# A fused two-layer attention and mixture-of-experts kernel: eleven tiles of the second expert layer get a table of their own and start before the last router groups are finished

## The chip, the cores and the metric

One core of a Trainium2 chip runs the whole kernel. The metric is the device time of one execution in microseconds (us). Three executions of the kernel before took 702.17, 703.75 and 704.6 us, a median of 703.75 us.

## The reference

32 sequences of 128 tokens with 128 features go through two layers. Each layer is a gated cross-attention (16 heads) and a gated mixture of 8 experts, both on a layer-normed copy of the running sum `x`:

```python
x = x + tanh(g_xattn[0]) * L0_xattn(layernorm(x), ctx, ...)
x = x + tanh(g_ffn[0])   * L0_ffn(layernorm(x), ...)         # one expert per token
x = x + tanh(g_xattn[1]) * L1_xattn(layernorm(x), ctx, ...)
x = x + tanh(g_ffn[1])   * L1_ffn(layernorm(x), ...)         # two experts per token

# L1_ffn
probs = softmax(xt @ gate_w.T); top_w, top_i = top_k(probs, 2)
top_w = top_w / (top_w.sum(-1) + 1e-9)
h = gelu(xt @ w1[e] + b1[e]); out_e = h @ w2[e] + b2[e]      # 128 -> 512 -> 128
out = sum over the two chosen experts of top_w * out_e
```

The change is about the last two lines of `x`: the end of the second attention and the second expert layer. A token's two experts are known only when its attention is done, and rows of one expert are computed together.

## The kernel before

The kernel is written by hand for the five engines; every engine has its own program, in order, and semaphores join them. Nothing is scheduled by a planner.

**Attention slots.** The batch is cut into 16 pairs of sequences. `pair_slots` runs slots p = -4, -3, ... and in slot p each engine does one step of several pairs: maxima of the scores of pair p+1 (TensorE, VectorE), scores and exponentials of pair p, values of pair p-1, the division, the new `x` and its statistics for pair p-2 (VectorE; the reciprocal root of the variance on GpSimd, L599 to L602), and for pair p-3 the normalised copy N (ScalarE, L717), its transpose (L824) and the router's logits (L954, L765). The second layer's slots run to p = 20, so slots 17 to 20 only bring the last pairs home.

**Router groups.** `GROUPS` cuts the pairs into six groups. A group's routing (`choose`, steps 0 to 19 on VectorE, `rank_group` on TensorE, one exponential on ScalarE) gives every token the two rows (SLOT) at which it stands among its experts' rows. GpSimd then writes the rows there with one indirect DMA for each 128 tokens and choice, `dispatch` (L628), 64 in all, to the tensor `dispatched`.

**The table.** After the last group `tables_by_first_row` (VectorE, L1389 to L1426, with three steps on TensorE) makes the list of 39 tiles of 256 rows: first row (TBL 0), expert (TBL 1) and the number of groups that must have been stored (TBL 2). The tiles are ordered by the group that fills their first row.

**Expert slots.** `tile_slots` runs slots i = -2 to 39. In slot i TensorE transposes the rows of tile i+1 (L824), does the hidden layer of tile i (L1057) and the output layer of tile i-1 (L1074). SyncE loads a tile's rows (L503) when its groups are stored. ScalarE copies the transposed rows (L791) and does gelu (L802). VectorE copies the weights (L1573), makes the rows' addresses and weights (L1580 to L1588), and for the output y adds the bias (L1598) and scales by the router's weight (L1601, twice). GpSimd sends y back by two indirect DMAs (L663). Transposed rows and y alternate between two PSUM banks each. At the end the rows are fetched back for chunks of tokens, summed (L1622) and added to x (L1625).

## Time and profile before

| | us |
|---|---|
| median of three executions | 703.75 |
| the profiled execution | 701.35 |
| its span in the profile | 699.5 |
| TensorE busy | 554.2 (79%) |
| VectorE busy | 507.9 (73%) |
| ScalarE busy | 359.4 (51%) |
| GpSimd busy | 308.2 (44%) |

A row of busy times gives the stretch, its length, then busy us (and instructions) of PE, PEld, DVE, ACT and POOL, the granted clock, the DMA share and GB/s. A row of the timeline gives start, duration, engine, source line, operation, output and inputs, and in brackets the idle time before it with what ended it. PEld is TensorE's weight load, SPq the DMA queue of SyncE. PEclk is the granted clock of TensorE as a share of 2.4 GHz. The execution lies 1.85 us above its own span and 2.4 us below the median.

### The profile page before, as it was taken

How to read it: one execution, taken by the hardware profiler on the slowest of the kernel's cores; microseconds unless marked ns; L12 is line 12 of the kernel's file. 1: busy time of each engine (PE TensorE's matmuls, PEld its weight loads, DVE VectorE, ACT ScalarE, POOL GpSimd, SP SyncE). 2: the span in 40 equal slices, each digit the busy share in tenths (PEclk: the TensorE clock that was granted, in tenths of full speed). 3: DMA queues.
4: the chain of work that ended last, by engine and by line, in shares of the span. 5: the costliest groups of instructions: out<-in, count | busy, mean ns of one | idle time of the engine just before them, and what ended most of it. 6: DMA issues, size and time to landing. Idle time of an engine off the chain costs nothing.

```text
span 699.5 us, 17510 instructions
## 1 busy us (share of the span) xinstructions
PE 554.2 (79%) x5770; PEld 452.3 (65%) x5770; DVE 507.9 (73%) x1617; ACT 359.4 (51%) x860; POOL 308.2 (44%) x431
## 2 busy tenths in 40 slices
PE   6789999998840118997779989898843999999991
PEld 4667777776630007886656767676532999999991
DVE  5998889888348884553789999999755555666662
ACT  2177777776723104551256767677721555555550
POOL 5512233221110017755664225575777445555553
PEclk9899999999975557999989999999975999999996
DMA  5354434433010002342546545442113222344333
GB/s 179 89 142 132 138 108 140 148 110 85 19 56 22 0 4 75 107 97 80 147 144 182 164 147 169 140 119 85 42 43 93 66 77 68 119 145 126 109 126 105
DMA packets 99864, 72.59 MB, mean 104 GB/s; under 512 B 13272, under 2 KB 93272, under 8 KB 99752
## 3 DMA queue, kind: packets, MB, share of 16 engines
q1 hardware_dynamic: 88496, 53.64, 26.3%
q0 software_dynamic: 6816, 14.10, 6.7%
q10 hardware_dynamic: 4464, 3.73, 1.8%
q8 instruction: 48, 0.79, 0.5%
q14 instruction: 40, 0.33, 0.2%
HBM read 42.14 MB, written 29.85 MB: 103 GB/s over the span
## 4 chain that ended last, share of the span: by engine, by line
PE 54%; DVE 22%; issue 9%; ACT 5%; DMA 4%; POOL 3%; SPq 1%; POOLq 0%; DVEq 0%; ACTq 0%
PE bank L1057 14%; PE bank L1074 10%; PE bank L824 7%; DVE MX L1247 5%; PE bank L861 5%; PE bank L992 5%; PE bank L845 4%; PE bank L1067 3%; DVE PT L1478 2%; ACT OT L760 2%; PE bank L941 2%; ACT XT_HL_WR L736 2%; DVE XN L1290 1%; PE bank L908 1%; PE bank L897 1%
## 5 line engine op out<-in xcount | busy, mean ns | idle before, releaser
L703 ACT ACTIVATE PT<-bank 128x512 f32<-128x512 f32 x256 | 151.9, 597 | 92.2 <-PE bank L845 91.7
L1247 DVE TENSOR_REDUCE MX<-bank 128x4 f32<-128x512 f32 x256 | 172.5, 680 | 20.1 <-PE bank L861 18.0
L861 PE MATMUL bank<-KS,QS_N 96*128 96x128 f16 x1024 | 102.9, 224 | 12.5 <-DVE MX L1247 7.2
L663 POOL DMA_INDIRECT returned<-PT,META_ROW x78 | 79.4, 1018 | 66.4 <-DVE PT L1601 54.2
L1057 PE MATMUL bank<-XGT,XT_HL_WR 128*128 128x256 f32 (+1 forms) x468 | 103.5, 359 | 1.6 <-issue 1.0
L861 PEld LDWEIGHTS bank<-KS,QS_N 96*128 96x128 f16 x1024 | 76.0, 102 | 35.7 <-DVE MX L1247 14.5
L845 PE MATMUL bank<-QS_N,KS 98*128 98x512 f16 x256 | 97.5, 386 | 0.7 <-ACT PT L703 0.3
L1057 PEld LDWEIGHTS bank<-XGT,XT_HL_WR 128*128 128x128 f32 x468 | 79.5, 198 | 14.1 <-issue 7.2
L1074 PEld LDWEIGHTS bank<-WALL,HT 128*128 128x128 f32 x624 | 75.6, 192 | 2.6 <-issue 0.6
L628 POOL DMA_INDIRECT dispatched<-N,SLOT x64 | 63.3, 989 | 31.2 <-issue 15.1
L1074 PE MATMUL bank<-WALL,HT 128*128 x624 | 76.1, 275 | 0.2 <-issue 0.2
L802 ACT ACTIVATE HT<-bank,XT_HL_WR 128x256 f32<-128x256 f32 x156 | 63.9, 471 | 21.4 <-PE bank L1057 21.4
L791 ACT ACTIVATE XGT<-bank 128x128 f32<-128x128 f32 (+1 forms) x78 | 25.8, 330 | 94.6 <-PE bank L824 90.8
L992 PE MATMUL bank<-PT,VA 128*32 128x128 f32 x2048 | 70.2, 278 | 0.1
L650 POOL DMA_INDIRECT PT<-normed,LIST x39 | 37.8, 969 | 71.3 <-DVE LIST L1546 59.8
L1573 DVE COPY XT_HL_WR<-WALL 128x512 f32 (+1 forms) x78 | 35.3, 453 | 42.2 <-issue 27.5
L992 PEld LDWEIGHTS bank<-PT,VA 128*32 128x32 f32 x2048 | 52.7, 111 | 18.0 <-issue 11.5
L599 POOL TENSOR_SCALAR MINUS<-MV_N 128x2 f32<-128x2 f32 x32 | 7.6, 237 | 120.9 <-DVE MV_N L1130 120.6
L1598 DVE TENSOR_TENSOR PT<-bank,WALL 128x256 f32<-128x256 f32 x39 | 16.6, 425 | 42.6 <-PE bank L1074 42.6
L615 POOL DMA_INDIRECT HT<-returned,SLOT x32 | 31.6, 989 | 18.4 <-DMA returned<-PT 9.8
L824 PE MATMUL bank<-CONST,PT 128*128 128x128 f32 x117 | 27.2, 288 | 11.1 <-issue 5.1
L717 ACT ACTIVATE N<-X,OFFSET_N,RSTD_N 128x128 f32<-128x128 f32 x64 | 27.8, 483 | 7.9 <-POOL OFFSET_N L602 7.8
(240 smaller groups left out, 994.1 us busy)
## 6 DMA issues: line engine op xcount, KB each, us to landing
spread<-XT_HL_WR SPq DMA_DIRECT2D x96, 128.0 KB
QS_N<-spread SPq DMA_DIRECT2D x128, 48.0 KB
KS<-spread SPq DMA_DIRECT2D x32, 192.0 KB
PT<-dispatched SPq DMA_DIRECT2D x39, 132.0 KB, 2.1
WALL<-in_w SPq DMA_DIRECT2D x8, 578.0 KB
CT<-in_ctx SPq DMA_DIRECT2D x32, 128.0 KB, 2.6
returned<-PT SPq DMA_DIRECT2D x39, 64.0 KB
WALL<-in_w ACTq DMA_DIRECT2D x8, 256.0 KB, 2.8
```

What stands on the lines that cost most here:

```text
L628: pool.indirect_dma_start(xs[:, :], bass.IndirectOffsetOnAxis(ap=SLOT[:, k, b:b + 1], axis=0), N[:, b, :], None).then_inc(SCAT[d.s], 16)
L650: pool.indirect_dma_start(XG6[:, i % 6, 0:D], None, normed[:, :], bass.IndirectOffsetOnAxis(ap=LIST[:, i:i + 1], axis=0)).then_inc(XA[i % ...
L663: pool.indirect_dma_start(ys[1][:, :], bass.IndirectOffsetOnAxis(ap=META_ROW[:, a.f, c:c + 1], axis=0), YS[:, a.f, c, :], None).then_inc(S ...
L703: nc.scalar.activation(PT[:, c, 4 * g:4 * g + 4, :].rearrange("p j q -> p (j q)"), ST[i % 2][:, :], ACT.Exp, scale=SCALE[layer]).then_inc( ...
L802: last = nc.scalar.activation(HT[:, a.u, m, :], bank[2 * a.u + m // 2][:, TILE * (m % 2):TILE * (m % 2) + TILE], ACT.Gelu, bias=WR[:, a.t, ...
L824: return nc.tensor.transpose(to, of, ident[0:n, 0:n])
L845: nc.tensor.matmul(ST[i % 2][:, :].rearrange("p (j q) -> p j q", j=J), KS[0:98, x.r, g, c * P:(c + 1) * P], QS[0:98, x.r, J * g:J * g + J, ...
L861: last = nc.tensor.matmul(MB[i % 2][:, j * P:(j + 1) * P], QS[0:96, m.r, J * g + j, c * P:(c + 1) * P], KS[0:96, m.r, g, c * P:(c + 1) * P ...
L992: last = nc.tensor.matmul(PA[32 * g:32 * g + 32, 256 * c + P * (j // 2):256 * c + P * (j // 2) + P], VA[:, b.r, c, head(g, j), :], PT[:, c ...
L1057: last = nc.tensor.matmul(bank[2 * a.u + m // 2][:, n * (m % 2):n * (m % 2) + n], WR[:, a.t, m * P:(m + 1) * P], XGT[:, a.u, 0:n], start=T ...
L1074: last = nc.tensor.matmul(bank[6 + a.u][:, c * D:(c + 1) * D], HT[:, a.u, m, c * P:(c + 1) * P], WALL[:, bass.ds(r + (W1COLS[1] + m * D), ...
L1247: V.tensor_reduce(out=MX[:, m.u, 2 * J * g + c:2 * J * (g + 1):2], in_=MB[i % 2][:, :].rearrange("p (j k) -> p j k", j=J), op=ALU.max, axi ...
```

## The change

1. The second layer's attention slots end at p = 16. What stood in slots 17 to 20 (normalised copy, transpose and logits of the last two pairs, the last pair's division, routing of groups 4 and 5) is run by a function `drain(i)` of each engine ahead of expert slots -2 to 9.
2. The groups are (0,3), (3,3), (6,3), (9,2), (11,3), (14,2). The first three groups fill at least 11 whole tiles (`EARLY`). These have their own table, made in attention slots 15 and 16 from the counts of three groups. The other 28 tiles' table is made in `drain(7)` to `drain(9)`. SyncE waits for groups 0 to 2 before tile 0 and for all before tile 11.
3. GpSimd writes the 12 blocks of group 4 before the first y and the 8 blocks of group 5 behind the y of tile 1.
4. In slots 15 and 16 the statistics of pair p-2 move ahead on VectorE, and ScalarE normalises a pair at the end of the slot in which its statistics are made.
5. ScalarE scales y in place of VectorE, one slot later; y has one PSUM bank (PA) and the transposed rows have one (PG), where there were two each.
6. TensorE and VectorE load the table's register ahead of the slot's waits.

```diff
-GROUPS = ((0, 3), (3, 3), (6, 3), (9, 3), (12, 2), (14, 2))
+GROUPS = ((0, 3), (3, 3), (6, 3), (9, 2), (11, 3), (14, 2))
+EARLY_GROUP = 2
+IN_SLOTS = 4
+EARLY = -(-(sum(GROUPS[EARLY_GROUP]) * 4 * P - E * (TILE - 1)) // TILE)
-            for p in range(-4, PAIRS + (3, 5)[layer]):
+            for p in range(-4, PAIRS + (3, 1)[layer]):
 # SyncE, second_experts
+                sp.wait_ge(av_done, 4 * PAIRS - 1)
                 sp.wait_ge(tables_ready, 2)
+                stored_groups(0, EARLY_GROUP + 1)
                 for i in range(TILES[1]):
+                    if i == EARLY:
+                        sp.wait_ge(tables_ready, 3)
+                        stored_groups(EARLY_GROUP + 1, len(GROUPS))
-                    sp.wait_ge(groups_done, need)
 # GpSimd, second_experts
-                confirm(Group(len(GROUPS) - 1))
+                deviations(LAST)
+                rest_of_stores(4, 0, 12)
                 for i in range(TILES[1]):
-                    pool.wait_ge(y_kept, a.g + 1)
+                    if i == 2:
+                        rest_of_stores(5, 0, 8)
+                    pool.wait_ge(y_scaled, i + 1)
 # ScalarE
+            def drain(i):
+                if i == -2:
+                    keep_transposed(BEFORE_LAST)
+                if i == 0:
+                    shares(Group(4))
+                    keep_logits(BEFORE_LAST)
+                if i == 1:
+                    normalise(LAST)
+                if i == 2:
+                    keep_transposed(LAST)
+                if i == 3:
+                    keep_logits(LAST)
+                if i == 5:
+                    shares(Group(5))
+            def scaled(a):
+                act.wait_ge(y_kept, a.g + 1)
+                for c in range(2):
+                    last = nc.scalar.activation(YS[:, a.f, c, :], YS[:, a.f, c, :], ACT.Copy, scale=META_W[:, a.f, c:c + 1])
+                last.then_inc(y_scaled, 1)
 # TensorE
+                    if layer == 1 and p == PAIRS - 1:
+                        table_order(0)
                     scores_for_maxima(7)
                     scores(a, 3)
...
+            def drain(i):
+                if i == -2:
+                    transposed(BEFORE_LAST)
+                if i == 0:
+                    logits(1, BEFORE_LAST)
+                if i == 1:
+                    rank_group(Group(4))
+                if i == 2:
+                    transposed(LAST)
+                if i == 3:
+                    logits(1, LAST)
+                if i == 6:
+                    rank_group(Group(5))
+                    table_counts(1)
+                if i == 8:
+                    table_order(1)
+                if i == 9:
+                    table_rows(1)
-                        pe.wait_ge(y_kept, before(a.g - 1))
+                        pe.wait_ge(y_kept, before(a.g - 1 + layer))
-                                    last = nc.tensor.matmul(bank[6 + a.u][:, c * D:(c + 1) * D], HT[:, a.u, m, c * P:(c + 1) * P],
+                                    last = nc.tensor.matmul(PA[:, c * D:(c + 1) * D], HT[:, a.u, m, c * P:(c + 1) * P],
 # VectorE
+            def drain(i):
+                if i == -1:
+                    steps(4, range(7))
+                if i == 0:
+                    divide(1, LAST)
+                    add_attention(LAST)
+                    second_stats(LAST)
+                    steps(4, range(7, 11))
+                if i == 1:
+                    steps(4, (11, 13, 14, *WEIGHTS))
+                if i == 4:
+                    steps(5, range(7))
+                if i == 5:
+                    steps(5, range(7, 12))
+                if i == 6:
+                    steps(5, (13, 14, *WEIGHTS))
+                if i == 7:
+                    table_keys(1)
+                if i == 8:
+                    table_values(1)
+                    table_places(1)
+                if i == 9:
+                    table_columns(1)
-                        for c in range(2):
-                            last = V.tensor_scalar(out=YS[:, a.f, c, :], in0=YS[:, a.f, c, :], scalar1=META_W[:, a.f, c:c + 1],
-                                                   scalar2=None, op0=ALU.mult)
```

Where the instructions stand, in three places. First TensorE between the attention and the first expert tiles. `PLACE,VALUES` is the table, `N` the normalised copy, `WG,NT` the logits, `MASKG` and `SHARE` the ranks of a group, `CONST,PT` the transposes of a tile's rows, `XGT` a hidden layer. Before:

```order
L954 MATMUL bank<-WG,NT 128x8 x2
L978 MATMUL bank<-MASKG,BEFORE 128x32
L979 MATMUL bank<-SHARE,ONES 128x32
L981 MATMUL bank<-MASKG,ONES 128x32
L981 MATMUL bank<-MASKG,ONES 128x24
L981 MATMUL bank<-MASKG,ONES 128x16
L981 MATMUL bank<-MASKG,ONES 128x8
L1031 MATMUL bank<-MASKG,ONES 128x56
L824 MATMUL bank<-CONST,ONE 128x128
L1037 MATMUL bank<-PLACE,VALUES 128x39 x4
L824 MATMUL bank<-CONST,PT 128x128 x4
L1057 MATMUL bank<-XGT,XT_HL_WR 128x256 x4
```

Now, from the last values of the attention on:

```order
L1058 MATMUL bank<-PT,VA 32x128 x16
L901 MATMUL bank<-CONST 128x128 x3
L896 MATMUL bank<-CONST,OT 128x128 x4
L896 MATMUL bank<-CONST,N 128x128 x2
L896 MATMUL bank<-CONST,PT 128x128 x2
L1075 MATMUL bank<-WG,NT 128x8 x2
L896 MATMUL bank<-CONST,PT 128x128 x2
L1190 MATMUL bank<-XGT,XT_HL_WR 128x256 x4
L1083 MATMUL bank<-MASKG,BEFORE 128x48
```

The first hidden layer has moved ahead of the ranks of groups 4 and 5 and of the whole table; the transpose of pair 14's copy N stands directly before the first tile's rows.

Second, GpSimd at the same place (`MINUS` to `OFFSET_N` are the four small steps of one pair's normalisation). Before, all of it from the last two normalisations:

```order
L602 TENSOR_TENSOR OFFSET_N<-MINUS,RSTD_N 128x2
L628 DMA dispatched<-N,SLOT 34816x132 x6
L599 TENSOR_SCALAR MINUS<-MV_N 128x2
L600 TENSOR_SCALAR VE_N<-MV_N 128x2
L601 TENSOR_TENSOR RSTD_N<-VE_N,EXPO 128x2
L602 TENSOR_TENSOR OFFSET_N<-MINUS,RSTD_N 128x2
L628 DMA dispatched<-N,SLOT 34816x132 x22
L663 DMA returned<-PT,META_ROW 18176x128 x78
```

Now, from pair 14's normalisation on:

```order
L590 TENSOR_TENSOR OFFSET_N<-MINUS,RSTD_N 128x2
L644 DMA dispatched<-N,SLOT 34816x132 x2
L587 TENSOR_SCALAR MINUS<-MV_N 128x2
L588 TENSOR_SCALAR VE_N<-MV_N 128x2
L589 TENSOR_TENSOR RSTD_N<-VE_N,EXPO 128x2
L590 TENSOR_TENSOR OFFSET_N<-MINUS,RSTD_N 128x2
L644 DMA dispatched<-N,SLOT 34816x132 x12
L688 DMA returned<-PT,META_ROW 18176x128 x4
L644 DMA dispatched<-N,SLOT 34816x132 x8
L688 DMA returned<-PT,META_ROW 18176x128 x74
```

The last 20 blocks now stand around the y of tiles 0 and 1; group 3's are all ahead of the last normalisation.

Third, ScalarE in expert slots 4 to 6 (`HT` gelu, `PT<-PT,META_W` the scaling, `EXG` the exponential of group 5), where there were only copies and gelu:

```order
L853 ACTIVATE XGT<-bank 128x256
L877 ACTIVATE PT<-PT,META_W 128x128 x2
L866 ACTIVATE HT<-bank,XT_HL_WR 128x256 x4
L809 ACT_TABLE_LOAD
L809 ACTIVATE EXG<-SHX 128x36
L853 ACTIVATE XGT<-bank 128x256
L877 ACTIVATE PT<-PT,META_W 128x128 x2
L866 ACT_TABLE_LOAD
L866 ACTIVATE HT<-bank,XT_HL_WR 128x256 x4
```

Two loads of ScalarE's tables and the scalings have come in between the gelus.

## Rows read from the trace of the kernel before

**Rows 1.** Page, part 2: 40 slices of the span, tenths

```profile
PE   6789999998840118997779989898843999999991
PEclk9899999999975557999989999999975999999996
```

**Rows 2.** Busy time by engine in slot 14, the hand-over and the expert loop

```profile
486.00:494.30 8.30, 7.32 (x112) 5.06 (x111) 7.11 (x17) 6.01 (x13) 6.08 (x9) 1.00 0.14 45
...
506.80:537.70 30.90, 9.28 (x70) 7.48 (x67) 18.38 (x96) 4.29 (x13) 23.38 (x27) 0.62 0.18 58
543.60:685.50 141.90, 141.90 (x992) 133.94 (x992) 85.93 (x343) 75.24 (x186) 76.44 (x76) 1.00 0.35 106
```

**Rows 3.** Chain of waits in order of time, 506 to 534 us

```profile
506.94 1.07 POOL dispatched L628
...
533.21 2.14 DMA PT<-dispatched
```

**Rows 4.** Timeline of PE: attention slots 14 to 16, first tiles, steady state

```profile
486.06 0.27 PE L824 MATMUL bank<-CONST,MX 128*32 128x128 f32 x1
...
494.33 0.27 PE L824 MATMUL bank<-CONST,MX 128*32 128x128 f32 x1
...
500.31 0.38 PE L845 MATMUL bank<-QS_N,KS 98*128 98x512 f16 x1
...
508.26 0.60 PE L824 MATMUL bank<-CONST,OT 128*128 128x128 f32 x4
...
537.72 3.62 PE L1057 MATMUL bank<-XGT,XT_HL_WR 128*128 128x256 f32 x8
...
541.54 1.89 PE L1057 MATMUL bank<-XGT,XT_HL_WR 128*128 128x256 f32 x8
543.60 2.05 PE L1074 MATMUL bank<-WALL,HT 128*128 x16 [0.17 <-issue]
...
566.09 1.95 PE L1074 MATMUL bank<-WALL,HT 128*128 x16
567.88 0.38 PE L824 MATMUL bank<-CONST,PT 128*128 128x128 f32 x2
```

**Rows 5.** Timeline of POOL from slot 14 on

```profile
488.37 1.09 POOL L628 DMA_INDIRECT dispatched<-N,SLOT  x1 [0.56 <-issue]
489.76 0.96 POOL L628 DMA_INDIRECT dispatched<-N,SLOT  x1 [0.30 <-issue]
...
494.71 0.24 POOL L599 TENSOR_SCALAR MINUS<-MV_N 128x2 f32<-128x2 f32 x1 [0.20 <-DVE MV_N L1130]
...
496.11 0.19 POOL L602 TENSOR_TENSOR OFFSET_N<-MINUS,RSTD_N 128x2 f32<-128x2 f32 x1
```

**Rows 6.** Timeline of DVE: table, then one expert slot

```profile
524.57 0.21 DVE L1389 COPY BASE<-bank 128x56 f32<-128x56 f32 x1
...
528.02 0.16 DVE L1402 SCALAR_TENSOR_TENSOR ONE<-ONE 128x1 f32<-128x1 f32 x1
...
529.76 0.25 DVE L1415 TENSOR_SCALAR PLACE<-CONST,ONE 128x39 bf16<-128x39 f32 x1
...
531.33 0.20 DVE L1422 TENSOR_SCALAR TBL<-bank 128x39 int32<-128x39 f32 x1
...
564.46 0.42 DVE L1598 TENSOR_TENSOR PT<-bank,WALL 128x256 f32<-128x256 f32 x1 [1.06 <-PE bank L1074]
```

**Rows 7.** Granted clock, 1 us windows: fall and rise

```profile
514.00:515.00 1.00, 0.00 (x0) 0.00 (x0) 0.83 (x4) 0.00 (x0) 0.78 (x4) 0.60 0.16 55
...
541.00:542.00 1.00, 1.00 (x6) 0.81 (x5) 0.00 (x0) 0.99 (x4) 0.80 (x1) 0.74 0.70 189
```

**Rows 8.** Timeline of ACT: a normalised copy, and the load of gelu's table

```profile
516.02 0.88 ACT L717 ACTIVATE N<-X,OFFSET_N,RSTD_N 128x128 f32<-128x128 f32 x2 [3.21 <-POOL OFFSET_N L602]
...
539.72 1.28 ACT L802 ACT_TABLE_LOAD   x1 [1.37 <-PE bank L1057]
541.01 1.57 ACT L802 ACTIVATE HT<-bank,XT_HL_WR 128x256 f32<-128x256 f32 x4
```

More of the change, by code:

```diff
@@ L997, in attention_slot, with transposed, logits @@
                 return slot
+            def transposed(y):
+                pe.wait_ge(n_copied, y.g + 1)
+                pe.wait_ge(lg_kept, y.g)
+                for c in range(2):
+                    last = transpose(PF[:, 256 + c * P:256 + (c + 1) * P], N[:, y.b + c, 0:D])
+                last.then_inc(n_t, 1)
+            def logits(layer, y):
+                pe.wait_ge(n_kept, y.g + 1)
+                for c in range(2):
+                    last = nc.tensor.matmul(PF[:, 256 + E * c:256 + E * c + E], NT[:, c * P:(c + 1) * P],
+                                            WG[:, layer, :], start=True, stop=True)
+                last.then_inc(lg_done, 1)
@@ L1078, in expert_layer @@
                 pe.wait_ge(tables_ready, layer + 1)
-                tile_slots(layer, slot)
+                tile_slots(layer, slot, None, drain if layer else None)
             for layer in range(2):
@@ L1228, in slot @@
                     m, a, b, z, f, n = pair(1), pair(0), pair(-1), pair(-2), pair(3), pair(4)
+                    late = layer == 1 and p >= PAIRS - 1
                     def low_halves():
@@ new lines, in table_columns @@
+            def table_columns(part):
+                first, n = PARTS_OF_TILES[part]
+                these = slice(first, first + n)
+                chain.sync()
+                dve.wait_ge(ordered, part + 1)
+                read = (PG, PF)[part]
+                start, expert, filled = (read[:, 2 * P + k * n:2 * P + (k + 1) * n] for k in range(3))
+                link(V.tensor_copy(FILLED[:, 0, these], filled))
+                link(V.scalar_tensor_tensor(out=STARTF[:, these], in0=start, scalar=float(TILE), in1=FILLED[:, 0, these], op0=ALU.mult, op1=ALU.add))
+                link(V.tensor_copy(TBL[:, 0, these], STARTF[:, these]))
+                if part == 0:
+                    link(V.tensor_copy(TAKEN[:, :], read[:, 3 * P:3 * P + E]))
+                V.tensor_scalar(out=TBL[:, 1, these], in0=expert, scalar1=float(WCOLS[1]), scalar2=None,
```

395 lines of the change are left out of this document (238 added, 157 removed).

## The prediction

> **What bounds the kernel now.** I read the page first, then busy times by stretch, then the chain of waits, then each engine's timeline around the place that the change touches. The page's slices show TensorE nearly full in both attention layers and in the last quarter, with a hole between the second attention and the second expert layer, in which its clock also falls [rows 1]. The stretches put numbers on it: between the last values of the attention (506.8) and the first hidden layer (537.7) TensorE is busy 9.28 of 30.9 us at a granted clock of 0.62; from the first output layer (543.60) to the last (685.5) it is busy 141.90 of 141.90 us at 1.00 [rows 2]. So the expert loop is TensorE's: each of the 39 tiles is an output layer of 1.78 us (566.09 to the transposes at 567.88 [rows 4]), two transposes and a hidden layer, 3.73 us in all (141.9 us for 38 rounds), and nothing taken from another engine there shortens it. The hole belongs to a chain: in it GpSimd's dispatches and normalisations, then routing and table on VectorE, then SyncE's load of the first rows, which lands at 535.35 [rows 3]. What the change can win is the hole, some 31 us plus the slow start behind it.
>
> **When the first tiles can start.** I follow the new order engine by engine, with durations of before.
>
> Slot 14 gets group 3's routing, 14 small VectorE steps. VectorE is busy 7.11 of 8.3 us there [rows 2]; at some 0.2 us a step 2.0 of the 3 us fill idle time or overlap, and I take 0.8 us more for the slot. Bounds: 0 and 3.
>
> Slot 15 gets the early table. `table_keys` took 3.6 us (524.57 to 528.18) and `table_values` and `table_places` 1.8 (to 530.01) [rows 6]. VectorE's other work ahead of it in that slot (the split of the maxima, division, new x, statistics, weights of group 3: 15 instructions of 0.15 to 0.5 us) is some 4 us by my estimate, so the keys end 7.6 us after the slot's start at 494.33 [rows 4], at about 502 on the old clock. TensorE has `table_order(0)` in front of the last pair's scores 3, which ran at 500.31 [rows 4]: a new wait of about 2 us, behind which stand ScalarE's exponentials.
>
> The later wait is GpSimd's. Counting from its first dispatch of slot 14 at 488.37, 16 dispatches and the normalisations of pairs 12, 13 and 14 now stand in front of pair 14's OFFSET_N: 6 + 8 + 2 dispatches of 1.26 us (0.96 and 0.30 of issue) are 20.2 us, three normalisations of 1.7 us (494.71 to 496.30 and a start) are 5.1 [rows 5]. That is 513.7, where before the same step was done just ahead of the dispatch at 506.94 [rows 3]: group 3's eight dispatches were moved ahead of it. TensorE needs this copy before the first tile's rows, as the new order shows. The rows themselves are there: the early table's places are made in slot 15 and its columns, 1.3 us, behind two steps of TensorE in slot 16, by my estimate at about 508.7; from a finished table (531.53 [rows 6]) it was 1.7 us to SyncE's issue at 533.21 and 2.14 more to the landing [rows 3]: 512.5.
>
> From 513.7: ScalarE's copy 0.9 [rows 8], two transposes of N 0.45, two of the rows 0.4, ScalarE's copy of both 0.8, the logits 0.5, the next transposes 0.4; hidden layer 0 starts at about 516.9. Then 1.73, the ranks of group 4 0.5, transposes 0.4, hidden layer 1 1.73: the first output layer would start at 521.2 at full clock. But TensorE is idle for over 3 us before it and thin before that. In the run of before the transposes of 508.26 [rows 4] were the last work but for short bursts, and the clock went to 1.2 GHz inside 514 to 515; it came back inside 541 to 542, 4 us into steady work [rows 7], and hidden layer 0 took 3.62 us there where the next took 1.89 [rows 4]. I take half of some 4 us for it, 2.0 (bounds 0 and 4): 523.2. Against 543.60 the start is **20.4 us earlier**.
>
> **What the loop gets in return.** TensorE is full there, so everything it is given counts: one pair's transposes 0.45, its logits 0.5, ranks and counts 0.8, the table's two steps 0.6: **2.3 us**.
>
> VectorE waits 1.06 us for TensorE in a tile of before [rows 6] and is rid of the scaling, 0.5 us: about 1.5 us to spare. The drains of slots 4 and 5 fit (7 and 5 steps, 1.6 and 1.2 us); that of slot 6 (8 steps behind the ranks) leaves it 0.8 late. Slot 7 gives it 17 steps, 3.9 us, and slot 8 another 2.0. An output layer may be late only by what lies between the add that frees the y bank (564.46 + 0.42) and the next output layer (566.09), 1.2 us [rows 4, 6]. What is over is a stall of TensorE in slots 8 and 9: 3.9 + 0.8 - 1.5 - 1.2 is 2.0, less the 0.4 that TensorE itself loses there: **1.6 us** (bounds 0 and 4).
>
> Tile 11 is the seam. Its load waits for the late table and for group 5. The table is ready one us into `drain(9)`; SyncE's 1.5 and the transfer's 2.2 follow, and against TensorE's own need in slot 10 this is **2.9 us** late. GpSimd runs beside it to nearly the same end: group 4 may start at 521.3, 12 dispatches are 15.1, y of tiles 0 and 1 5.0, group 5 10.1: 551.5 and a landing of 1.5 at the most beyond the instruction (a load takes 2.14 from its issue), where the table is ready at about 555. Then y of tile 2 goes, and tile 10's addresses wait for it (eight buffers): 555.6, just in time.
>
> Costs taken at nothing: ScalarE's scaling (0.7 us a tile in an engine busy 75.24 of 141.90 us [rows 2]; if that cover went, gelu would be late and the price be per tile); register loads ahead of waits (TensorE has no gap to give back); one bank for the transposed rows (ScalarE's copy is done 1.5 us before the next transposes); the two loads of ScalarE's tables around group 5's exponential. For these the row shows 1.28 us, gelu right behind it at 541.01 [rows 8]: slot 5 then takes ScalarE 1.28 + 0.23 + 0.38 + 0.7 + 1.28 + 1.64 = 5.5 us, and it has 6.1 to 6.7 before TensorE wants the gelu. The Trainium skill, page "ScalarE: Activation LUTs", section "What ACT_TABLE_LOAD costs", speaks against this: every switch costs 2.66 us, for about 1.38 us of draining goes with the load. By that page slot 5 would take ScalarE some 8.3 us and TensorE would lose about 2 more. Before the one load in this trace no such drain shows.
>
> At the end ScalarE's scaling stands where two VectorE steps stood: 0.2 us.
>
> **Sum.** 20.4 - 2.3 - 1.6 - 2.9 - 0.2 = 13.4 us. The profiled execution was 701.35, so its like would be 688.0; the median of the runs shown stands 2.4 above it, and from 703.75 the forecast is **690.3 us**.
>
> **The rivals.**
>
> *Less is lost at the seam* (0.18). If the clock does not fall and VectorE's steps overlap as they do between the maxima, 2.0 and some 3 of the 4.5 us of stalls stay: 18.4 us, 685.3. For it: short steps cost little behind long ones. Against it: all steps in the drains depend on each other.
>
> *GpSimd's queue takes the seam* (0.23). Twenty dispatches and four y are 30 us in front of tile 2's y. Anything that makes them 0.2 us longer each, or starts group 4 later, comes out at tile 10's addresses and again in slots 11 and 12, while VectorE is held in order; ScalarE's dearer table switches belong here too. At 5 us: 695.3.
>
> *One bank for y* (0.05, the slower side). VectorE's add stands behind weights and addresses (1.85 us) in its slot. If gelu, behind ScalarE's new scaling, releases the weights so late that the add always comes those 1.85 us later, the next output layer waits 0.65 us in every tile: 39 tiles are 25 us, 715. It turns the sign from an add that comes 1.55 us late (1.2 of cover and 13.4 / 39). Against it: ScalarE is idle for half of each tile.
>
> *The early tiles do not start early* (0.04). If a wait in the new order ties tile 0 to something late, the last pair's work for instance, the hole stays and only its filling moves: 703, no change.
>
> **How the numbers follow.** 0.50 for the forecast, within about 687 to 694 by the bounds of the slot, the clock and the stalls. The range runs from the mean of the better case less a us to the seam case plus 2: 684 to 697.5; it leaves out the last two cases and the tails. A difference within 0.3% (2.1 us) cannot be told from none. Faster 0.91, same 0.04, slower 0.05.
>
> **What would show it.** Right: the first output layer at 520 to 525 of the span; N's copy of pair 14 released by GpSimd at about 514, with dispatches in a row before it; TensorE without a gap in the loop except 1 to 2 us around slots 8 and 9 (released by VectorE's add) and some 3 us before tile 11's transposes (released by the load of its rows); 3.73 us a tile from tile 12 on. Wrong: gaps in every tile; a first tile after 530; a stall of over 5 us at tile 10 or 11; or no stall there at all.

## The result, and the profile after

The changed kernel took 686.48, 689.23, 692.8 and 693.06 us, a median of **691.01 us**; four runs of the kernel before, 701.12 to 704.6, have a median of 702.96. The ratio is 0.9829 with a 95% interval of 0.9802 to 0.9857: faster by 12 us, where 690.3 was forecast. The profiled execution is the one of 692.8 us, 1.8 above the median. The page of the changed kernel, lines that answer to [rows 1] and the two groups of the expert loop:

```profile
span 691.1 us, 17399 instructions
...
PE   6789999999861106987769998899879989999991
...
PEclk8789999999995555999889999999968999999996
...
PE 49%; DVE 19%; issue 10%; ACT 7%; POOL 7%; DMA 7%; SPq 1%; POOLq 0%; ACTq 0%; DVEq 0%
...
L1190 PE MATMUL bank<-XGT,XT_HL_WR 128*128 128x256 f32 (+1 forms) x468 | 102.1, 356 | 0.2 <-issue 0.2
...
L1212 PE MATMUL bank<-WALL,HT 128*128 x624 | 76.7, 276 | 1.0 <-DVE PT L1826 1.0
```

The hole in TensorE's row has shrunk to a dent (8, 7), and a thin place of the loop has come in its stead. Busy times of slot 14, slot 16 and the loop from the first output layer to the last (they answer to [rows 2]):

```profile
489.10:498.10 9.00, 7.66 (x118) 5.19 (x117) 8.72 (x30) 6.24 (x14) 6.90 (x10) 1.00 0.15 49
507.50:518.50 11.00, 9.69 (x89) 6.51 (x87) 5.88 (x27) 5.11 (x12) 7.81 (x12) 0.50 0.27 75
526.30:676.50 150.20, 145.23 (x1010) 136.12 (x1008) 72.24 (x327) 100.35 (x271) 93.29 (x96) 0.99 0.36 108
```

Slot 14 opens with the transposes of the maxima at 489.12; before, it opened at 486.06. The three us are lost near the kernel's start, which the change does not touch: the third pair of the first attention layer has its maxima transposed at 49.69 us, before at 46.38, and the granted clock of 34 to 52 us is 0.86, before 1.00. This part differs from one execution to the next: in the profiles of the first four variants below slot 14 opens between 482.7 and 491.3. So I compare **from slot 14's start**:

| us | before | after | difference |
|---|---|---|---|
| slot 14's start to the first output layer (543.60; 526.28) | 57.54 | 37.16 | -20.38 |
| first output layer to the end of the last (685.51; 676.52) | 141.91 | 150.24 | +8.33 |
| from there to the end | 14.0 | 14.6 | +0.6 |
| slot 14's start to the end | 213.4 | 202.0 | -11.4 |

The hand-over in the timelines of PE, ACT, DVE and POOL (start, duration, engine, line, operation, in brackets the idle time ahead of it and what ended it):

```profile
506.25 0.32 PE L896 MATMUL bank<-CONST,ONE 128*128 128x128 f32 x1 [1.89 <-DVE ONE L1605]
...
514.12 1.93 PE L1058 MATMUL bank<-PT,VA 128*32 128x128 f32 x32 [0.69 <-ACT PT L728]
...
517.43 1.06 PE L896 MATMUL bank<-CONST,OT 128*128 128x128 f32 x4
518.58 0.66 PE L896 MATMUL bank<-CONST,N 128*128 128x128 f32 x2
...
521.05 3.20 PE L1190 MATMUL bank<-XGT,XT_HL_WR 128*128 128x256 f32 x8
...
517.61 0.88 ACT L793 ACTIVATE N<-X,OFFSET_N,RSTD_N 128x128 f32<-128x128 f32 x2 [0.89 <-POOL OFFSET_N L590]
...
512.01 0.17 DVE L1647 COPY FILLED<-bank 128x11 f32<-128x11 f32 x1 [3.73 <-PE bank L1111]
...
515.87 0.24 POOL L587 TENSOR_SCALAR MINUS<-MV_N 128x2 f32<-128x2 f32 x1 [0.54 <-DVE MV_N L1268]
...
517.38 0.20 POOL L590 TENSOR_TENSOR OFFSET_N<-MINUS,RSTD_N 128x2 f32<-128x2 f32 x1
...
527.23 1.09 POOL L644 DMA_INDIRECT dispatched<-N,SLOT  x1 [3.38 <-DVE N L1336]
```

ScalarE's copy of pair 14 waits for GpSimd, as forecast, and ends at 518.49. But TensorE, which is to transpose that copy, has only just finished its own work: its transposes at 518.58 stand behind others that also ended at 518.49. The clock had gone to 1.2 GHz behind the wait for the table's order at 506.25, and slot 16 took 11.0 us where it took 7.2 before. Two paths end together here. They are not quite apart either: GpSimd's dispatches were done at 515.34, and it then waited 0.54 us for pair 14's statistics, which VectorE could make only after its own wait of 3.73 us for TensorE's slow slot (512.01).

The seam, first in PE's timeline, then in the chain of waits, then in the view of the dispatching line:

```profile
552.44 0.32 PE L896 MATMUL bank<-CONST,ONE 128*128 128x128 f32 x1 [0.99 <-DVE ONE L1605]
...
554.89 2.05 PE L1212 MATMUL bank<-WALL,HT 128*128 x16 [0.18 <-DVE PT L1826]
...
558.83 1.95 PE L1212 MATMUL bank<-WALL,HT 128*128 x16
563.76 0.44 PE L896 MATMUL bank<-CONST,PT 128*128 128x128 f32 x2 [2.98 <-DMA PT<-dispatched]
564.04 3.01 PE L1190 MATMUL bank<-XGT,XT_HL_WR 128*128 128x256 f32 x8
566.84 2.54 PE L1212 MATMUL bank<-WALL,HT 128*128 x16
```

```profile
556.58 4.08 DMA dispatched<-N,SLOT
...
561.59 2.13 DMA PT<-dispatched
```

```profile
DMA to landing us min/median/max: 2.3/2.3/4.1
```

Group 5's last dispatch was issued at 556.58 and landed 4.08 us later, where the median from issue to landing is 2.3: SyncE could load tile 11 only then. TensorE waited 2.98 us and then ran its next hidden layer at half clock for part of the way (3.01 instead of 1.89, the output layer 2.54 instead of 1.95).

### The profile page after: what moved, and what is told of

It reads as the page before. It is cut to its first block, busy times and chain, and to the rows that moved or that the text cites. A ratio compares the mean times of both kernels' runs of the same rounds, so it can differ in the third digit from the quotient of the medians.

```text
span 691.1 us, 17399 instructions
## 1 busy us (share of the span) xinstructions
PE 554.3 (80%) x5751; PEld 453.2 (66%) x5751; DVE 487.8 (71%) x1575; ACT 383.4 (55%) x940; POOL 307.9 (45%) x431
## 3 DMA queue, kind: packets, MB, share of 16 engines
q10 hardware_dynamic: 4464, 3.73, 1.9%
## 4 chain that ended last, share of the span: by engine, by line
PE 49%; DVE 19%; issue 10%; ACT 7%; POOL 7%; DMA 7%; SPq 1%; POOLq 0%; ACTq 0%; DVEq 0%
PE bank L1190 9%; PE bank L1212 8%; PE bank L896 7%; PE bank L1058 6%; PE bank L934 5%; DVE MX L1396 5%; PE bank L917 5%; POOL dispatched L644 3%; DMA PT<-normed,LIST 2%; DVE PT L1708 2%; POOL PT L672 2%; ACT OT L781 2%; PE bank L1020 2%; ACT XT_HL_WR L761 2%; ACT PT L728 1%
## 5 line engine op out<-in xcount | busy, mean ns | idle before, releaser
L934 PE MATMUL bank<-KS,QS_N 96*128 96x128 f16 x1024 | 103.3, 225 | 14.6 <-DVE MX L1396 8.5
L1190 PE MATMUL bank<-XGT,XT_HL_WR 128*128 128x256 f32 (+1 forms) x468 | 102.1, 356 | 0.2 <-issue 0.2
L688 POOL DMA_INDIRECT returned<-PT,META_ROW x78 | 77.6, 994 | 51.5 <-ACT PT L877 36.3
L917 PE MATMUL bank<-QS_N,KS 98*128 98x512 f16 x256 | 99.2, 392 | 0.5 <-ACT PT L728 0.5
L1212 PEld LDWEIGHTS bank<-WALL,HT 128*128 128x128 f32 x624 | 76.3, 193 | 3.6 <-issue 1.6
L1212 PE MATMUL bank<-WALL,HT 128*128 x624 | 76.7, 276 | 1.0 <-DVE PT L1826 1.0
L1058 PE MATMUL bank<-PT,VA 128*32 128x128 f32 x2048 | 72.4, 284 | 0.7 <-ACT PT L728 0.7
L1058 PEld LDWEIGHTS bank<-PT,VA 128*32 128x32 f32 x2048 | 54.2, 113 | 19.8 <-issue 11.5
L738 ACT ACTIVATE XT_HL_WR<-bank 128x256 f32<-128x256 f32 x32 | 12.1, 379 | 35.7 <-PE bank L896 35.7
```

The costliest lines, as they stand in the source:

```text
L688: pool.indirect_dma_start(ys[1][:, :], bass.IndirectOffsetOnAxis(ap=META_ROW[:, a.f, c:c + 1], axis=0), YS[:, a.f, c, :], None).then_inc(S ...
L917: nc.tensor.matmul(ST[i % 2][:, :].rearrange("p (j q) -> p j q", j=J), KS[0:98, x.r, g, c * P:(c + 1) * P], QS[0:98, x.r, J * g:J * g + J, ...
L934: last = nc.tensor.matmul(MB[i % 2][:, j * P:(j + 1) * P], QS[0:96, m.r, J * g + j, c * P:(c + 1) * P], KS[0:96, m.r, g, c * P:(c + 1) * P ...
L1058: last = nc.tensor.matmul(PA[32 * g:32 * g + 32, 256 * c + P * (j // 2):256 * c + P * (j // 2) + P], VA[:, b.r, c, head(g, j), :], PT[:, c ...
L1190: last = nc.tensor.matmul(bank[2 * a.u + m // 2][:, n * (m % 2):n * (m % 2) + n], WR[:, a.t, m * P:(m + 1) * P], XGT[:, a.u, 0:n], start=T ...
L1212: last = nc.tensor.matmul(PA[:, c * D:(c + 1) * D], HT[:, a.u, m, c * P:(c + 1) * P], WALL[:, bass.ds(r + (W1COLS[1] + m * D), D)], start= ...
```

## The experiments

All of them are the changed kernel with the edit named, but for one. Columns: the kernel before on the same chip (median), the kernel (median), the ratio with its interval, and from the profile the first output layer after slot 14's start, the loop from there to the last output layer's end, and slot 14's start to the end, each a difference of two starts or ends in PE's timeline (the end is the span's). The ratio and its interval are those on record; they need not equal the quotient of the two medians.

| run | before | this | ratio | first y | loop | slot 14 to end |
|---|---|---|---|---|---|---|
| (after) | 703.0 | 691.0 | 0.983 | 37.2 | 150.2 | 202.0 |
| e1_warm | 702.2 | 686.6 | 0.9751 (0.9712 to 0.9789) | 37.1 | 147.0 | 198.6 |
| e2_stats_first | 702.2 | 689.0 | 0.9782 (0.9742 to 0.9823) | 37.1 | 147.3 | 198.7 |
| e3_warm_stats | 702.2 | 682.3 | 0.9727 (0.9695 to 0.9758) | 32.6 | 148.1 | 194.8 |
| e4_group4_early | 702.2 | 686.8 | 0.9771 (0.9750 to 0.9792) | 39.3 | 146.8 | 200.5 |
| e0_again | 752.0 | 753.7 | 0.9986 (0.9951 to 1.0021) | 44.6 | 178.1 | 237.5 |
| e5_group5_early | 752.0 | 748.9 | 0.9947 (0.9916 to 0.9978) | 44.7 | 177.1 | 236.3 |
| e7_group5_later | 752.0 | 747.8 | 0.9941 (0.9912 to 0.9970) | 44.8 | 176.3 | 235.7 |
| e6_all | 752.0 | 749.4 | 0.9958 (0.9925 to 0.9991) | 48.9 | 174.2 | 237.3 |
| b0_before | 757.7 | 758.1 | 0.9986 (0.9955 to 1.0017) | 81.7 | 143.4 | 239.1 |
| e9_all_again | 757.7 | 751.1 | 0.9914 (0.9882 to 0.9947) | 47.9 | 176.0 | 238.2 |
| e8_vector_scales | 760.3 | 764.9 | 1.0082 (1.0047 to 1.0116) | 47.2 | 187.0 | 248.0 |
| e10_best | 760.3 | 753.3 | 0.9911 (0.9879 to 0.9942) | 46.8 | 177.6 | 238.8 |

The runs of the variants fell on four chips. On the one of the first four the kernel before takes 702 us, as in the result (whose own chip is not on record); on the other three 752 to 760. The two kinds are read apart. Each of these chips was used in one stretch of time only, so the record cannot part a property of the chip from one of the hour; "chip" below stands for both.

### Two paths to the first tile

```diff
+ if layer == 1 and p == PAIRS - 1: stay_busy(MB[0], 4)      # ahead of transposed(y)
+ if layer == 1 and p == PAIRS - 1: stay_busy(MB[0], 7)      # ahead of table_order(0)
+ if ending: stay_busy(MB[0], 2)                             # at two places of slot 16
```

> The changed kernel with 15 more filler matmuls of TensorE in slots 15 and 16 (4 ahead of the transposes of N, 7 ahead of the early table's order, 4 in slot 16), so that it is not idle while it waits. In the profile after, the granted clock goes to 1.2 GHz at about 506.6, slot 16 takes 11.0 us where the same slot took 7.2 before, and the first hidden layer takes 3.20 us where the next takes 1.89. Theory (the clock is part of the hand-over): with fillers the clock stays at 1.00 there, slot 16 takes 7 to 8 us and the first hidden layer 1.89; but pair 14's OFFSET_N, which came at 517.58, is set by GpSimd's row of dispatches and stays 28.5 us after slot 14's start, so the first output layer comes 34.5 to 35.5 us after that start instead of 37.2: 1.7 to 2.7 us gained, no more. Rival A (TensorE's slow slot alone sets the hand-over): the first output layer comes at 32 to 33.5, 4 to 5 us gained, with GpSimd released earlier too. Rival B (the fall has nothing to do with the idle time): slot 16 still runs at half clock and nothing changes, or the fillers cost their 15 times 0.3 us.

The clock stayed full through slot 16 (busy times of 507 to 516 us, the clock is the figure 1.00 behind POOL's 7.08), and TensorE was ready at 514.0. It then stood still until the copy came (PE's timeline):

```profile
507.00:516.00 9.00, 5.95 (x95) 4.49 (x93) 5.44 (x25) 4.00 (x9) 7.08 (x10) 1.00 0.28 80
```

```profile
513.36 0.66 PE L896 MATMUL bank<-CONST,OT 128*128 128x128 f32 x4
517.70 0.66 PE L896 MATMUL bank<-CONST,N 128*128 128x128 f32 x2 [3.69 <-issue]
...
520.17 3.44 PE L1196 MATMUL bank<-XGT,XT_HL_WR 128*128 128x256 f32 x8
```

OFFSET_N came 27.9 us after slot 14's start (28.3 in the profile after), and GpSimd had no wait in front of this normalisation, so its row held the time, as the theory said. My number was still too good: behind an idle stretch of 3.69 us the first hidden layer ran at half clock after all, and the first output layer came at 37.1, not 34.5 to 35.5. No gain at the hand-over. (The medians of this run and of the next lie 4.4 and 2.1 us under the 691.0 of the result. That does not come from the hand-over; the late landing at the seam, which the profile after has and theirs have not, is worth 3.3 to 3.4 us there, slot 14 to the end. How many of the result's unprofiled executions had it is not known.)

```diff
- if layer == 1 and (p, u) == (PAIRS, 1): table_columns(0)
+ if layer == 1 and (p, u) == (PAIRS, 2): table_columns(0)   # behind pair 14's statistics
- for k, b in older[0:1] if a else older[0:2] if ahead else older:
+ for k, b in older[0:1] if a else [] if ahead else older:   # and all of them behind deviations(z)
```

> The changed kernel with the two things in front of pair 14's OFFSET_N taken out of its way: VectorE's division, addition and statistics of pair 14 stand ahead of the reading of the early table (they stood behind it, and behind 3.73 us of idle time until 512.01), and GpSimd's two dispatches of slot 16 stand behind the deviations instead of ahead. Theory (GpSimd's row and TensorE's slow slot tie): OFFSET_N comes 2.5 to 3 us earlier against slot 14's start (28.5 us after it in the profile after), but TensorE works through slot 16 at half clock until 518.5 as before, so the first output layer stays within 0.5 us of 37.2 us after slot 14's start, and the time does not change. Rival (GpSimd's row alone set the hand-over, as the prediction had it): the first output layer comes 2.5 to 3 us earlier.

```profile
516.60 0.25 POOL L590 TENSOR_TENSOR OFFSET_N<-MINUS,RSTD_N 128x2 f32<-128x2 f32 x1
...
519.63 1.06 PE L896 MATMUL bank<-CONST,OT 128*128 128x128 f32 x4
520.48 0.64 PE L896 MATMUL bank<-CONST,N 128*128 128x128 f32 x2
```

OFFSET_N came 25.3 us after the start, 3.0 earlier, and TensorE's transposes still stood behind its own half-clock slot: 37.1 again. With both edits:

> Both edits of the two experiments before (fillers in slots 15 and 16; pair 14's statistics and deviations ahead of the table's reading and of two dispatches). Theory (two paths of nearly equal length end at pair 14's transposes): only together do they give their full worth; the first output layer comes 4 to 6 us earlier against slot 14's start (31.5 to 33 instead of 37.2), more than the sum of 1.7 to 2.7 and 0 that each gives alone. Rival (one path): together they give no more than the better of the two. The time of the whole follows only in part, since tile 11 waits for GpSimd's stores and the late table: if group 4's first dispatch does not come earlier by as much, the stall of 2.98 us at tile 11 grows.

```profile
509.41 0.41 PE L896 MATMUL bank<-CONST,N 128*128 128x128 f32 x2 [1.30 <-issue]
...
511.01 1.89 PE L1196 MATMUL bank<-XGT,XT_HL_WR 128*128 128x256 f32 x8
...
515.34 1.84 PE L1218 MATMUL bank<-WALL,HT 128*128 x15
```

32.6 us: each edit alone is worth 0.1 us at this place, and the two together 4.5. That is what two paths of equal length look like. Of it 3.9 arrive at the end of the profile (slot 14 to end 194.8, against 198.7 for the two single edits; the intervals of the ratios of e1 and e3 overlap, so the times alone do not show this step). At 682.3 us **this version beats both kernels** on a chip like the first: its ratio, 0.9695 to 0.9758, lies under the 0.9802 to 0.9857 of the change.

### The seam at tile 11

None of these three touched the seam, and in none did the stores hold it. The chain of waits in the first of them, then PE's wait:

```profile
558.34 0.20 DVE TBL L1658
...
559.38 2.12 DMA PT<-dispatched
```

```profile
561.54 0.44 PE L896 MATMUL bank<-CONST,PT 128*128 128x128 f32 x2 [1.43 <-DMA PT<-dispatched]
```

The late table was written at 558.5, SyncE issued 0.85 us later, and TensorE waited 1.43 us (1.29 and 1.42 in the next two) with no loss of clock behind it. Group 4 earlier:

```diff
 if i == -1:
     steps(4, range(7))
+    divide(1, LAST); add_attention(LAST); second_stats(LAST); steps(4, range(7, 11))
- if i == 1: steps(4, (11, 13, 14, *WEIGHTS))
+ if i == 0: steps(4, (11, 13, 14, *WEIGHTS))    # TensorE's ranks in slot 0 too
```

> The changed kernel with group 4's routing one slot earlier (VectorE makes all eleven steps and the last pair's division in slot -1, TensorE its ranks in slot 0, VectorE its weights there), so that GpSimd's 12 dispatches start 3 to 4 us earlier than 527.23 against slot 14's start (38.1 us after it). In the profile after, group 5's last dispatch ends at 557.54, its landing is waited for until about 561.5, and the late table is ready at 559.2: tile 11 stalls TensorE 2.98 us. Theory (group 5's stores and their landing end last at tile 11): the stall falls to 1 to 2 us, where the late table binds instead, and 1 to 2 us are gained, a little more if the clock does not dip. Rival (the late table binds already, as the prediction had it): the stall stays at 3 us. The rank group ahead of the first hidden layer costs at most 0.5 us.

GpSimd's last store of group 5 ended 3.06 us ahead of the table's ready time (554.58 and 557.64); in e1, where group 4 was not moved, this was 1.65 us. The wait hardly changed, 1.25 us for 1.43. The theory had named 1 to 2 us too, but the three runs without the edit have it as well, so the number does not speak for it. The rival said that the late table binds already, as the prediction had it, and **the late table binds** in these four profiles, though at less than the rival's 3 us. The stores' margin is thin in the unmoved order: by the median of 2.3 us the last store of the profile after (556.58) would have landed 0.3 us ahead of the table, which was ready at 559.2, and one late landing was enough. The price was at the hand-over, 39.3 us: the ranks wait 0.84 us for VectorE, and the first two hidden layers, at half clock for longer, take 3.62 and 2.43 us (3.20 and 1.89 in the profile after).

```profile
517.88 0.22 PE L1083 MATMUL bank<-MASKG,BEFORE 128*128 128x48 bf16 x1 [0.84 <-DVE MASKG L1306]
```

### Three other chips

> The changed kernel unaltered, for a second profile of the seam and more times. In the profile after, group 5's last dispatch was issued at 556.58 and SyncE was released by its landing only 4.08 us later, so tile 11 waited 2.98 us and the clock dipped to 0.58 behind it (1.9 us more). In four variants that left the seam as it was, or moved group 4 alone, the late table released SyncE instead and the wait was 1.25 to 1.43 us with no dip. Theory (the late landing is an accident of one execution, and the late table is the usual bound): a wait of 1.3 to 1.5 us, y of tile 9 5.2 to 5.4 us behind that of tile 8, and 198 to 199 us from slot 14's start to the end where the profile after has 202.0; median 687 to 691. Rival (in the unaltered order the stores are always last): 3 us and a dip again.

This run came to another chip. There the change gains nothing: ratio 0.9986. The hand-over is again far shorter than before's, but the first twelve output layers lose 35.4 us over 3.73 each. Rows of POOL, DVE, PE and ACT behind the eighth tile:

```profile
614.30 0.96 POOL L688 DMA_INDIRECT returned<-PT,META_ROW  x1 [0.31 <-issue]
...
616.66 0.42 DVE L1826 TENSOR_TENSOR PT<-bank,WALL 128x256 f32<-128x256 f32 x1 [13.47 <-remote]
...
617.33 2.07 PE L1212 MATMUL bank<-WALL,HT 128*128 x8 [13.57 <-issue]
...
617.99 0.38 ACT L853 ACTIVATE XGT<-bank 128x256 f32<-128x256 f32 x1 [16.88 <-remote]
```

GpSimd had run sixteen indirect DMAs without a pause, from 595.31 to 615.26, at its usual 1.26 us. From 603.8 on TensorE, VectorE and ScalarE did nothing for 12.9 us, and all three went on 1.4 us and more after GpSimd's row was over. Between slot 14 and the last output layer this profile has seven stretches of over 1 us in which none of the three works, some 23 us in all, each within a row of indirect DMAs or ending at most 2.5 us behind one. The profile after, on the faster chip, has a longer row, 48 indirect DMAs without a pause from 527.2 to 588.1, and no such stretch. The kernel before, on another of the slower chips:

> The kernel before, unaltered, for a second profile. The batch before this one ran on another chip, on which the kernel before took 752.0 us (median) and the changed one 753.7, and in the changed kernel's trace there VectorE, ScalarE and TensorE stood still for 5 to 14 us at a time (12.3 and 13.5 us ahead of the addition of y) while GpSimd ran rows of 8 to 24 indirect DMAs, 1.26 us each, without a pause; on the first chip the same rows stall nobody. Theory: on such a chip the kernel before loses its 50 us in the same way, in its own rows of dispatches and gathers, and the changed kernel loses more of it in layer 2, where the rows now stand beside the tiles. If this run comes to that chip again, the trace shows stalls of that kind in slots 13 to 16, and fewer than the changed kernel has behind its first output layer. If it comes to a chip like the first: 700 to 705 us, slot 14 opens within 483 to 490 us, and from it to the end it takes 213 to 214 us as in rows 2 and 4.

```profile
579.71 0.20 DVE L1422 TENSOR_SCALAR TBL<-bank 128x39 int32<-128x39 f32 x1 [1.20 <-DVE TBL L1421]
...
588.38 0.38 ACT L791 ACTIVATE XGT<-bank 128x256 f32<-128x256 f32 x1 [22.24 <-issue]
```

```profile
587.69 0.66 PE L824 MATMUL bank<-CONST,PT 128*128 128x128 f32 x2 [10.18 <-issue]
```

Its row of 22 dispatches stands in the hole, and so the loss does too: 81.7 us to the first output layer instead of 57.5, and then a loop of 143.4 with hardly a stall. VectorE's step at 579.71 waits 1.20 us for the step right before it, which on the first chip costs 0.2, and which is about one indirect DMA. The changed kernel saves 37 us at the hand-over there and gives 34.7 back in the loop (178.1 - 143.4); two of the slower chips are compared there. Slot 14 itself opens 33.8 us later than in the profile before (519.87 against 486.06), but not for a slowness of everything: in the first attention layer, in which GpSimd issues no indirect DMA, the last maxima are transposed at 182.01 against 178.99, and the changed kernel has 179.93 on the slower chip (e0) against 181.97 on the faster. That the rows cause the stalls is argued from where both stand, in either order of the kernel; no run took the rows away. The other variants on these chips:

> The changed kernel with group 5's routing and the late table one slot earlier on VectorE and TensorE (in front of the addition of y, where VectorE stands idle 1.6 to 2.1 us in slots 2 to 4), group 5's shares one slot earlier on ScalarE; GpSimd's order is not touched. Theory (at the seam the late table ends last by 1 to 1.7 us, GpSimd's last store right behind it): the wait at tile 11 changes from 1.4 us to that of the stores, 0 to 1.5 us by how late they land (last dispatch ends 30.3 us after group 4's first), so 0 to 1.4 us gained there; the 1.0 us stall ahead of the table's order moves one slot ahead and stays 1 to 2 us. Rival (the stores end last in any case): the wait at tile 11 is 2.5 to 3 us in this run too and nothing is gained.

> The changed kernel with GpSimd's order altered by one place: group 5's eight dispatches stand behind the stores of tiles 0, 1 and 2 instead of behind those of 0 and 1, so they end 2.53 us later (four indirect DMAs of 1.26 us would be two tiles; one tile is two). Nothing else moves. Theory (the table ends last by 1 to 1.7 us): the wait at tile 11 grows by 2.53 us less that margin plus what a landing takes beyond the instruction, from 1.4 to 2.5 to 4.5 us; where it passes some 2.5 us the clock dips behind it as in the profile after, 1 to 2 us more. Rival (stores not in the way): 1.4 us as in the others.

> All together: fillers in slots 15 and 16; pair 14's statistics and deviations first; group 4's routing one slot earlier; group 5's routing and the late table one slot earlier in front of the addition of y. Theory: the hand-over is that of fillers and statistics together (first output layer 32.6 us after slot 14's start) plus at most 1 us for group 4's ranks ahead of the first hidden layer; the wait at tile 11 (1.42 us in that run) goes to 0 to 0.5, for both of its sides come 2 to 5 us earlier; the stall ahead of the table's order stays 1 to 2 us, one slot earlier. From slot 14's start to the end 193 to 194.5 us, against 202.0 in the profile after and 194.8 with the first two edits; median 679 to 684. Rival (group 4's early routing costs as much at the hand-over as the seam gives back, as its 39.3 against 37.1 us suggests): 195 to 196 us.

> The kernel of all four edits once more (fillers, pair 14's statistics first, group 4's routing a slot earlier, group 5's routing and the late table a slot earlier), since its first run came to the slower chip. On a chip like the first: first output layer 32.6 to 34 us after slot 14's start, the wait at tile 11 0 to 0.5 us instead of 1.4, one stall of 1 to 2 us in slot 7, 193 to 194.5 us from slot 14's start to the end (202.0 in the profile after, 194.8 with the first two edits), median 679 to 684 us. Rival (group 4's early ranks cost at the hand-over what the seam gives back): 195 to 196 us from slot 14 and no gain over the first two edits. On the slower chip: no difference from the kernel before beyond 1%, as before.

Edits of the first two, for group 5: `steps(5, range(7))` from slot 4 to the place ahead of the addition of y in slot 3, and every later step likewise; `rest_of_stores(5, 0, 8)` at `i == 3` instead of `i == 2`. The third and fourth join the edits of fillers, statistics, groups 4 and 5. All four are 0.4 to 0.9% under the kernel before on their chip, and the stalls beside the rows (12.1 us ahead of one addition in e7, two of 5.4 and 7.2 in e5) cover the seam, so that their questions about tile 11 stay unanswered: neither theory nor rival can be read. e6 and e9 show that the kernel of all edits gains no more than 0.9% where the other engines stand still beside GpSimd's rows.

```diff
- V.tensor_tensor(out=YS..., op=ALU.add).then_inc(y_kept, 1)
+ link(V.tensor_tensor(out=YS..., op=ALU.add))
+ for c in range(2): last = V.tensor_scalar(out=YS[:, a.f, c, :], ..., scalar1=META_W[:, a.f, c:c + 1], op0=ALU.mult)
+ last.then_inc(y_kept, 1)                       # and ScalarE's scaled(a) removed
```

> The changed kernel with one part undone: the scaling of y by the gates' weights is back on VectorE (two steps of some 0.2 us behind the addition, GpSimd and the bank released by them) and gone from ScalarE; all else as changed. The prediction gave VectorE 0.5 us a tile for being rid of it and used this slack in slots 4 to 9, and took ScalarE's part at nothing. Theory: TensorE's 3.73 us a tile from tile 12 on do not change, for VectorE has 1.5 us to spare there; but the stalls of slots 8 and 9, 0.97 and 0.18 us in the changed kernel, grow by 0.4 to 1.0 us, since 17 steps of the late table stand in front of a longer chain; and the table itself comes 0.4 to 1 us later, which tile 11 feels in full. Together 1 to 2 us slower than the changed kernel, on a chip like the first. Rival (the scaling matters nowhere, or costs per tile): the same within 0.5 us from slot 14's start to the end, or some 3.9 us more for every 0.1 us a tile. On a chip like the second and third: within 1% of the kernel before.

> Fillers, pair 14's statistics first, and group 5's routing with the late table a slot earlier; group 4 stays where the change has it. On a chip like the first this is the kernel of the first two edits (first output layer 32.6 us after slot 14's start, wait at tile 11 1.42 us with the table ready 1.65 us after the last store was issued, 194.8 us from slot 14 to the end) with the table moved 3.7 us ahead. Theory (the late table bound the load of tile 11): the wait falls to what the stores leave, 0 to 0.8 us, and 193.4 to 194.5 us are left from slot 14; median 679 to 683. Rival (a landing takes as long as in the profile after, 3.1 us beyond the instruction): the wait stays or grows to 1.4 to 2.8 us, and nothing is gained. On a chip like the second and third: within 1% of the kernel before, the stalls beside GpSimd's rows moved but not gone.

Both ran on one of the three slower chips. With the scaling on VectorE the ratio is 1.0082, against 0.9986 for the change as it is on another such chip: a further 1%, 7 us. The loop is 187.0 us against 178.1, and the difference lies behind the seam as well: from the thirteenth output layer on most tiles take 3.74 to 4.25 us, 6.7 us more in all than with the change as it is, and 5.6 more than in e10, which ran on the same chip with the scaling on ScalarE (104.7 us from there to the end of the last output layer, against 99.1). PE's timeline there:

```profile
649.29 2.05 PE L1202 MATMUL bank<-WALL,HT 128*128 x16 [0.22 <-DVE PT L1819]
```

So on such a chip ScalarE's scaling pays; its worth on a chip like the first was not measured. The last variant's ratio is 0.9911; its hope, a shorter wait at tile 11, could not be read either.

## Why the prediction was right, and where it was not

**Slot 14** became 0.75 us longer (9.02 against 8.27); 0.8 was said. **The new wait in slot 15** is 1.89 us; about 2 was said.

**The first output layer** comes 20.4 us earlier, the forecast number. That exact agreement is luck, and its reason was half of the truth. "The later wait is GpSimd's" held: ScalarE's copy is released by OFFSET_N, which ended 28.5 us after slot 14's start against the 27.6 of the sum (513.7 less 486.06). But the clock was put only behind this wait, at 2.0 us, and it fell already in front of it, after the wait in slot 15, and made slot 16 3.8 us longer on TensorE. The prediction had this loss at nothing, and it cost nothing only because GpSimd's path ended at the same time: the two tie to 0.1 us, as the first three runs show. The 2.0 us behind them came out as 1.3 in the first hidden layer (3.20 against 1.89) and 0.9 in the transposes and logits ahead of it (from 518.58 to 521.05, against 509.41 to 511.01 in e3). From the end of OFFSET_N to the first output layer it was 8.7 us in all, where the sum had 9.5 (513.7 to 523.2): 0.9 us late in front and 0.8 too much behind cancel. (The sum also has a slip: its own steps from 513.7 give 517.15 for hidden layer 0, not 516.9.) The sign "520 to 525 of the span" was missed, at 526.28, by the 3.1 us of slot 14's later start.

**TensorE's extra work in the loop** was set at 2.3 us and is near 1.5: the intervals between output layers are 0.22, 0.40, 0.22 and 0.21 above 3.73 where it stands, and the one with the transposes of the order is 1.66 above, of which 1.17 are the two waits below. A step costs the loop less than its busy time, which the sum had counted: two transposes, 0.38 us busy together, make an interval 0.22 us longer. **VectorE's lateness** was set at 1.6 us in slots 8 and 9; it is 0.99 and 0.18, both around the eighth output layer (552.44 and 554.89).

**Tile 11**, set at 2.9 us, is the term that was mis-sized: 1.25 to 1.43 us in the first four variants. Of the 1.5 us too much 0.65 are SyncE's, which needs 0.85 us from the table to its issue and not 1.5; the rest was not split. In the profile after it is 2.98, which agrees with the sum by coincidence, through an event that the sum had not, a landing 1.8 us later than usual, and 1.7 us of clock behind it (3.01 - 1.89 and 2.54 - 1.95), for which the sum had nothing. That GpSimd runs to nearly the same end held, though by another sum: group 4 started 38.1 us after slot 14's start, not 35.2 (521.3 less 486.06), since VectorE's rows for the dispatches (the line with 3.38) were ready only then, and tile 10's addresses were not late for y of tile 2.

**One bank for y** was a rival of 25 us and costs next to nothing per tile: 1.0 us of waiting in all (L1212 on the page after), of which 0.82 at the very last tile, where no hidden layer stands between two output layers; the sum had nothing for it. **ScalarE's tables** in slot 5:

```profile
537.52 1.61 ACT L866 ACTIVATE HT<-bank,XT_HL_WR 128x256 f32<-128x256 f32 x4
539.15 1.28 ACT L809 ACT_TABLE_LOAD   x1
540.45 0.23 ACT L809 ACTIVATE EXG<-SHX 128x36 f32<-128x36 f32 x1
...
541.55 1.28 ACT L866 ACT_TABLE_LOAD   x1
542.84 1.57 ACT L866 ACTIVATE HT<-bank,XT_HL_WR 128x256 f32<-128x256 f32 x4
```

Each load starts within 0.03 us of the end of the work in front of it and is followed at once. The 2.66 us of the Trainium skill, page "ScalarE: Activation LUTs", section "What ACT_TABLE_LOAD costs", do not appear: a switch is 1.28 us here, and TensorE lost nothing by it (the interval up to the output layer that reads this gelu is 3.95 us, 3.73 and 0.22 for ranks). **The tail** is 0.6 us longer; 0.2 was said.

In all: -20.4 + 8.3 + 0.6 = -11.4 us in the profile against -13.4 forecast; without the late landing and its clock, as e1 and e2 have it at the same hand-over, -14.7. The forecast lay between. In the medians it is 690.3 against 691.0, closer than its parts: the profiled execution was forecast at 688.0 and took 692.8, 3.1 us of the difference for the later start of slot 14 and 2.0 for the terms. None of the rivals came true on this chip, and of the seam rival the trigger was named (anything that makes GpSimd's row end later) but not the landing. What the prediction did not see at all is that the gain depends on the chip: on the one slower chip on which the unaltered change ran it gained nothing (0.9986).

## What to carry to other kernels

When two engines' queues end at the same instruction, take both out of the way before judging either edit: alone each was worth 0.1 us here, together 4.5. Compare executions from an event just ahead of the changed code, since the unchanged start of this kernel alone moves by up to 9 us between executions. And a row of indirect DMAs that is moved beside other work should be tried on several chips: hidden on one, it took back the whole gain on another, and on the two others variants of the change kept at most 0.9%.

## What the runs showed of the hardware

- On three chips of four TensorE, VectorE and ScalarE stood still for up to 12.9 us at a time beside rows of indirect DMAs that GpSimd ran without a pause; GpSimd's own pace was the same 1.26 us. On the chip of the first variants a row of 48 stopped nobody. On the slower ones a wait for an engine's own last step took 1.20 us (b0). What exactly is blocked was not tried and stays open, as does whether shorter rows would cure it: e7, with one tile's stores between the rows, was 0.8% faster than the change as it is on the same chip (747.8 against 753.7).
- The granted clock fell to 1.2 GHz in TensorE's wait of 3.69 us (e1), just behind that of 2.98 us (the seam after), and just behind the one of 1.89 us ahead of the thin slot 16; behind waits of 1.30 us (e3) and 1.43 us (the seam in e1) the next layers ran at full clock. With four fillers and seven more in slot 15 that wait was 0.23 us, and with these and four in slot 16 the clock stayed at 2.4 GHz.
- An indirect store of the profile after took 2.3 us from issue to landing in the median and at most 4.1.
